# Four edits in the later stages of a six-stage transformer kernel: weight splits released earlier, a block FFN with one bank per output tile, a turned bias share, and a cross attention projected one tile later

## The reference, cut to what matters

```python
x = x + L0_xattn(layernorm(x), ctx, ctx)     # 16 heads over 1601 keys
x = x + L0_attn(layernorm(x))                # Mamba-2 like state space, 16 heads
x = x + L0_ffn(layernorm(x))                 # block-sparse FFN: below
x = x + L1_xattn(layernorm(x), ctx, ctx)     # one head: below
x = x + L1_attn(layernorm(x))                # causal self attention
x = x + L1_ffn(layernorm(x))                 # quantized FFN: below

# L0_ffn: 16 blocks of 128 hidden units, the 4 most probable of each row are kept
mask = one_hot(top_k(softmax(xf @ router_w.T + router_b), 4))
h = relu(where(mask[:, :, None], einsum('nd,ibd->nib', xf, w1b) + b1b, 0))
y = einsum('nib,dib->nd', where(mask[:, :, None], h, 0), w2b) + b2

# L1_xattn
q, k, v = query @ Wq + bq, key @ Wk + bk, value @ Wv + bv      # key = value = ctx
out = softmax(q @ k.T) @ v

# L1_ffn's weights, per block of 32 of their columns
s = max(max(abs(wb)) / 7, 1e-12);  w = clip(round(wb / s), -8, 7) * s
```

## Time and profile before

| | |
|---|---|
| device time, median of 3 runs | 1714.09 us (1713.84 to 1717.74) |
| the profiled execution: its own time | 1715.84 us |
| its span | 1714.1 us |
| PE / DVE / ACT / POOL busy, share of the span | 91% / 68% / 52% / 45% |
| end of state_space, start of block_ffn | 993.86 us |
| end of the last matmul of block_ffn | 1227.53 us |
| first instruction of the next stage | 1229.36 us |
| scores of two tiles of cross1_batches, starts at 1324.68 and 1342.05 us | 17.37 us apart |
| pause of PE between state_space and block_ffn's norm | 13.93 us |

### The profile page before, as it was taken

One profiled execution on the slowest core, in us unless ns is written; L12 is line 12 of the kernel. 1 busy time (PEld: TensorE's weight loads), 2 busy tenths in 40 slices (PEclk: granted clock), 3 DMA queues, 4 the chain that ended last, 5 costly groups with the idle time before them and its releaser, 6 DMA issues. The chain is left out here.

```text
span 1714.1 us, 33945 instructions
## 1 busy us (share of the span) xinstructions
PE 1559.1 (91%) x13873; PEld 813.7 (47%) x13982; DVE 1167.6 (68%) x1951; ACT 889.2 (52%) x1190; POOL 770.2 (45%) x384
## 2 busy tenths in 40 slices
PE   6999999999999999999799979978878989899469
PEld 3445555555555555555446453333534444444224
DVE  6688888888888888886646448987522233626981
ACT  1487777777777777776373025411211222326750
POOL 1477788888878887885204816642000000000000
PEclk9999999999999999999999969989999999999779
DMA  4589999999999999999713764558679935000001
GB/s 138 131 177 192 193 190 192 190 191 191 194 194 190 199 195 195 189 182 173 166 49 123 232 261 92 140 152 202 196 305 365 396 147 221 1 1 0 1 0 49
DMA packets 556678, 282.74 MB, mean 165 GB/s; under 512 B 482912, under 2 KB 534624, under 8 KB 553456
## 3 DMA queue, kind: packets, MB, share of 16 engines
q1 hardware_dynamic: 556528, 280.63, 69.0%
HBM read 138.74 MB, written 22.54 MB: 94 GB/s over the span
## 5 line engine op out<-in xcount | busy, mean ns | idle before, releaser
L572 POOL TENSOR_TENSOR x<-x_prob,x 128x1604 bf16<-128x1604 f32 x120 | 388.0, 3233 | 142.3 <-ACT x L737 142.3
L867 DVE TENSOR_REDUCE x_negmax<-x_score 128x1 f32<-128x1604 f32 x128 | 233.6, 1825 | 17.3 <-PE x_score L613 7.0
L727 ACT ACTIVATE x_prob<-x_score,x_negmax 128x1604 f32<-128x1604 f32 x128 | 204.8, 1600 | 25.8 <-DVE x_negmax L867 21.1
L596 PE MATMUL x_ring<-x_ctx_hi,wk_split 128*128 128x400 bf16 (+1 forms) x1024 | 216.2, 333 | 0.2 <-DVE x_kT L795 0.2
L596 PE MATMUL x_ring<-wv_split,x_ctx_hi 128*128 128x512 bf16 (+1 forms) x770 | 200.4, 379 | 9.6 <-issue 7.3
L795 DVE SCALAR_TENSOR_TENSOR x_kT<-x_ring,bk,x_kT 128x400 bf16<-128x400 f32 (+1 forms) x256 | 162.2, 634 | 31.8 <-ACT x_kT L716 23.8
L737 ACT CAST x<-x_prob 128x1604 bf16<-128x1604 f32 x120 | 182.9, 1525 | 0.0
L801 DVE TENSOR_TENSOR x_v<-x_ring,x_v 128x512 bf16<-128x512 f32 (+1 forms) x208 | 143.7, 691 | 52.9 <-ACT x_v L720 50.0
L716 ACT ACTIVATE x_kT<-x_ring,bk 128x400 bf16<-128x400 f32 (+1 forms) x196 | 116.3, 594 | 91.0 <-PE x_ring L596 90.0
L720 ACT CAST x_v<-x_ring 128x512 bf16<-128x512 f32 (+1 forms) x148 | 86.5, 585 | 96.8 <-PE x_ring L596 96.8
L596 PEld LDWEIGHTS x_ring<-x_ctx_hi,wk_split 128*128 128x128 bf16 x1024 | 93.9, 97 | 86.9 <-issue 19.7
(11 more groups left out here) (346 smaller groups left out, 2435.9 us busy)
## 6 DMA issues: line engine op xcount, KB each, us to landing
y_ctx<-in_ctx SPq DMA_DIRECT2D x16, 1664.0 KB, 10.4
y_ctxT<-in_ctxT SPq DMA_DIRECT2D x16, 1601.0 KB, 14.3
x_stage<-in_ctxT SPq DMA_DIRECT2D x48, 400.0 KB, 4.4
x_q_rows<-q_rows SPq DMA_DIRECT2D x64, 128.0 KB, 3.2
m_xT<-in_L_ffn_w SPq DMA_DIRECT2D x16, 512.0 KB, 4.5
ffn_w_parts<-m_xT SPq DMA_DIRECT2D x32, 256.0 KB, 2.6
x_stage<-in_ctxT SPq DMA_DIRECT2D x16, 401.0 KB, 5.0
f_w<-ffn_w_parts SPq DMA_DIRECT2D x4, 1024.0 KB, 8.5
```

What stands on the lines that cost most here:

```text
L572: pool.tensor_tensor(ph[:, g % 2, 1, 0:NKP], prob[:, g % 2, :], ph[:, g % 2, 0, 0:NKP], ALU.subtract).then_inc(pl_done, 1)
L596: last = pe.matmul(out_, lhs, rhs, start=(i == 0), stop=(i == len(steps) - 1))
L727: nc.scalar.activation(prob[:, g % 2, :].rearrange("p (c n) -> p c n", n=QW), scores, ACT.Exp, bias=nmax[:, g % 2:g % 2 + 1], accum_out=rs ...
L867: dve.tensor_reduce(nmax[:, pair % 2:pair % 2 + 1], scores, mybir.AxisListType.XY, ALU.max, negate=True).then_inc(max_done, 1)
```

## The change

Four edits, each in one stage.

1. In state_space POOL's split waits for the turned gates (`s_gT >= 2 * KD`), for which SP's loads already wait, and no longer for the 8 bias additions.
2. In block_ffn each output tile has a bank of its own: two that were free and the six of the hidden layer, each released when its last group was read. The first four output tiles wait for the first half of the low parts only. The next stage's weight products stand ahead of the last output tile. In Dequant POOL's multiply is gone. DVE rounds with one tensor_scalar (add, min) and one scalar_tensor_tensor (subtract, times scale). `EARLY` is 20, and the high and low parts of a later piece come one slot after its front instead of two.
3. In cross1_queries the bias share is turned by 8 small transposes into a column per tile (128x8), so that cross1_batches reads it without the loads `cqs`.
4. In cross1_batches `o` of a tile is turned after the next tile's scores (into the unused columns of `pv`), and projected after the next tile's first two turns. The addition to x moves with it, and the loop has one more step at its end.

```diff
 (state_space, gpsimd)
-            pool.wait_ge(s_xo, NT)
+            pool.wait_ge(s_gT, 2 * KD)
...
 (block_ffn)
+        out_banks = banks[0:2] + [hidden_banks[n % 6] for n in range(len(groups) - 6, len(groups))]
+        next_banks = [out_banks[n] for n in range(KD)]
...
-            dq.on_sync(sp, dq.EARLY + 6, late_weights)
+            dq.on_sync(sp, dq.EARLY + 3, late_weights)
...
-                for i in dq.fronts(n):
-                    dq.multiply_on_gpsimd(pool, i)
-            for i in range(dq.EARLY, dq.count):
-                dq.multiply_on_gpsimd(pool, i)
...
-            pe.wait_ge(s_hlo, len(groups))
-            for t in range(NT):
+            def output(t):
                 if t >= 2:
-                    pe.wait_ge(s_out, t - 1)
+                    pe.wait_ge(s_masked, len(groups) - 7 + t)
+                pe.wait_ge(s_hlo, len(groups) if t >= NT // 2 else NB)
...
+            def next_weights():
+                pe.wait_ge(s_late, 48)
+                pe.wait_ge(s_out, KD)
...
+            for t in range(NT - 1):
+                output(t)
+            next_weights()
+            output(NT - 1)
...
 (class Dequant)
-    EARLY = 17
+    EARLY = 20
...
     def turn_at(self, i):
-        return self.front_at(i) + 2
+        return self.front_at(i) + (2 if i < self.EARLY else 1)
...
-        dve.tensor_scalar(w, w, ROUND, None, ALU.add).then_inc(self.s_unit, 1)
-        dve.wait_ge(self.s_unit, 6 * i + 5)
-        dve.tensor_scalar(w, w, ROUND, 7.0, ALU.subtract, ALU.min).then_inc(self.s_unit, 1)
+        dve.tensor_scalar(w, w, ROUND, ROUND + 7.0, ALU.add, ALU.min).then_inc(self.s_unit, 1)
+        dve.wait_ge(self.s_unit, 5 * i + 5)
+        dve.scalar_tensor_tensor(blocks, blocks, ROUND, s.unsqueeze(2).broadcast_to([P, 512 // QB, QB]),
+                                 ALU.subtract, ALU.mult).then_inc(self.s_back, 1)
...
 (cross1_queries, tensor)
+            pe.wait_ge(s_row, 2)
+            for t in range(NT):
+                last = pe.transpose(banks[6][:, t:t + 1], row[:, P * t:P * t + P], ident[0:1, 0:1])
+            last.then_inc(s_col, 1)
...
 (cross1_batches, sync)
-                sp.dma_start(cqs[:, par:par + 1],
-                             cq[:, P * u:P * u + P] if one else cq[:, bass.ds(P * u, P)]).then_inc(cqs_in[par], 16)
...
 (cross1_batches, tensor: tile u)
+                if finish:
+                    pe.wait_ge(s_o, u - 1)
+                    for j in range(KC):
+                        last = pe.transpose(pv[:, CD + P * j:CD + P * j + P], o[:, P * j:P * j + P], ident[:])
+                    last.then_inc(s_to, 1)
...
                     turn(0)
                     turn(1)
+                if finish:
+                    pe.wait_ge(s_w, 16)
+                    pe.wait_ge(s_of, u - 1)
+                    if not (isinstance(u, int) and u == 2):
+                        pe.wait_ge(s_x, u - 2)
+                    for j in range(KC):
+                        last = pe.matmul(wb[:], oT[:, P * j:P * j + P], wv[:, j, :], start=(j == 0), stop=(j == KC - 1))
+                    last.then_inc(s_wo, 1)
...
                     product(2)
                     product(3).then_inc(s_pv, 1)
-                    pe.wait_ge(s_o, u)
-                    pe.wait_ge(s_tf, 5 * (u - 1) + 3)
-                    for j in range(KC):
-                        last = pe.transpose(tb[other][:, P * j:P * j + P], o[:, P * j:P * j + P], ident[:])
...
```

More of the change, by code:

```diff
@@ L1440, in _ @@
                 for j in range(KD):
-                    last = pe.matmul(banks[2 + a][:, 0:CD + 1], wqT[:, j, a * P:(a + 1) * P], wkb[:, j, :],
+                    last = pe.matmul(out_banks[KD][:, KC:KC + 1], wkb[:, j, CD:CD + 1].broadcast_to([P, P]), bq[:, j:j + 1],
                                      start=(j == 0), stop=(j == KD - 1))
                 last.then_inc(s_next, 1)
[L1444 to L1451, removed]
+            pe.wait_ge(w2_in, 16)
+            for t in range(NT - 1):
+                output(t)
+            next_weights()
+            output(NT - 1)
         @block.scalar
@@ L1770, in tile, with turn, product @@
                     last.then_inc(s_s, 1)
+                def turn(j):
+                    if j >= 2 or not (isinstance(u, int) and u == 1):
+                        pe.wait_ge(s_tf, 4 * (u - 1) + j - 1)
+                    for i, (k0, kw) in enumerate(TGROUPS[j]):
+                        last = pe.transpose(tb[j % 2][0:kw, P * i:P * i + P], prob[:, other, k0:k0 + kw], ident[:])
+                    last.then_inc(s_t, 1)
+                def product(j):
+                    pe.wait_ge(s_tf, 4 * (u - 1) + j + 1)
+                    for i, (k0, kw) in enumerate(TGROUPS[j]):
+                        for s in range(2):
+                            last = pe.matmul(pv[L * s:L * s + L, 0:CD], pT[0:kw, j, P * i + L * s:P * i + L * s + L],
+                                             cn[0:kw, other, s, 4 * j + i, :],
+                                             start=(j == 0 and i == 0), stop=(j == NTG - 1))
+                    return last
+                if finish:
[3 more added lines that the diff above has]
+                    last.then_inc(s_to, 1)
                 if products:
-                    other = 1 - par
                     n_in = 32 * ((u - 1) // 2 + 1) if isinstance(u, int) else 16 * (u + (1 if par else 0))
@@ L1804, in tile @@
                     product(3).then_inc(s_pv, 1)
-                    pe.wait_ge(s_o, u)
-                    pe.wait_ge(s_tf, 5 * (u - 1) + 3)
-                    for j in range(KC):
-                        last = pe.transpose(tb[other][:, P * j:P * j + P], o[:, P * j:P * j + P], ident[:])
-                    last.then_inc(s_t, 1)
-                    pe.wait_ge(s_tf, 5 * u)
-                    if not (isinstance(u, int) and u == 1):
-                        pe.wait_ge(s_x, u - 1)
-                    for j in range(KC):
-                        last = pe.matmul(wb[:], oT[:, P * j:P * j + P], wv[:, j, :], start=(j == 0), stop=(j == KC - 1))
-                    last.then_inc(s_wo, 1)
             each_tile(pe, tile)
@@ L1846, in _, with tile @@
         def _(dve):
-            def tile(u, par, scores, products):
+            def tile(u, par, scores, products, finish):
                 if scores:
```

137 lines of the change are left out of this document (60 added, 77 removed).

## The result

The changed kernel takes 1701.26 us, median of 7 runs, against 1714.09 us before. The ratio is 0.9925 (95% interval 0.9907 to 0.9943): 12.8 us faster, where 16.5 were forecast. The profiled execution has a span of 1702.1 us against 1714.1, at a clock of 0.962 against 0.965.

A forecast was written before the change was run, and what follows sets the result against it. PE, busy 91%, was taken as the bound, so gains come only where it stands still or runs slowly. Edits 1, 2, 3 and 4: 3.9+12.9-0.3+0 = 16.5 us off 1714.09, about 1697; own range 1692 to 1702, 8 in 10 within 1685 to 1707.

The forecast's parts named there:

- Rival B: End of state_space: additions beside POOL's splits lose 7.7 us and more, taking edit 1's 3.9; 1701 us, chance 0.15 including its opposite.
- the load stall: block_ffn: DVE's DMA wait behind the late weights, 5.9 us, was expected to stay.
- POOL's interference: block_ffn, early weight pieces: POOL's slowing of DVE, some 0.8 us per piece before, was put at 0.55.
- Rival D: block_ffn: scalar_tensor_tensor beside POOL loses 0.96 us in each of 20 pieces, 19 us in all; 1716.6 us, chance 0.05.
- R: cross1_batches: time from the products' end to the context's landing, taken as 20.0 us.
- W: cross1_batches: PE's own work per tile, taken as 16.0 us.
- T: cross1_batches: mean time per tile, (20.0+16.0)/2 = 18.0 us, against 17.37 before.
- the bound of 18.8: cross1_batches: slow bound for the tile period, making edits 3 and 4 together -6 us.
- rival C: cross1_batches: waits are worse (period 18.8 us, or the clock falls in each), 6 us more; 1703 us, chance 0.10.
- Rival A: cross1_batches: context loads are no limit, 393 GB/s only mirrors PE's pace; price +13 us, so 1684 us, chance 0.15.
- Rival E: Start of block_ffn: shorter pause holds PE's clock, 20.9 us at 0.50 shrink by up to 9; 1689 us, chance 0.10.

The follow-up runs named there:

- old_schedule: Changed kernel with only the weight-piece slots as before (17 early pieces, high and low parts two slots behind the front), new operations kept: 1713.47 us, ratio 0.9988.
- old_ops: Changed kernel with only the operations as before (two scalar operations on DVE, POOL's multiply), new slots kept: 1700.4 us, ratio 0.9911.
- undo_batches: Changed kernel with cross1_batches in its order of before, the bias-share column kept: 1691.6 us, ratio 0.986.
- early_contextT: Changed kernel, but SP issues the next tile's cT before waiting for the products that free cn: 1681.03 us, ratio 0.9798.

## Why the prediction was right or wrong

**The time** of 1697 was 4 us low; 1701.26 lies inside the forecast's own range of 1692 to 1702. Behind it stand one term that was wrong and one that was right for other reasons than given.

**Edit 1** was right in mechanism and size. The additions lost 8 times 1.07 = 8.6 us, above the 7.7 worked out from the earlier trace rows, and the stage's last addition came 5.8 us later against the 5.0 taken; the gain is 3.2 instead of 3.9. The rule of the Trainium skill that was weighed there (SBUF — State Buffer, "Who interferes with whom": the one issued first holds the shared ports for its whole instruction) agrees with this trace: 1515 to 2117 ns against 684, each addition ending 0.55 us behind the split that ran when it started, and no change where the operand lies in PSUM. Rival B, on which the prediction hung that rule, would have needed all 8.9: the rule gave the loss of an addition rightly, but part of it fell into DVE's idle time.

**Edit 2** came to 14.0 against 12.9, and the end was SP's, as said. PE's side was right: no wait, its end 216.5 us after the stage's start against 215.1 worked out. The step that failed is the load stall, carried over as 5.9 us because the late weights stay behind the same piece. The runs old_schedule and old_ops show that the stall hung on the slots: all 10 us of load waits go with the new ones. By the program's order the reason is that a slot of the four is freed by a piece's low part, which now stands one slot behind its front; that is argued, not tested by itself. DVE's last low part was 4 us earlier than worked out for it (at 1198.75), and SP took most of that back: its last store landed some 9 us later, at about 1207.8, instead of 6.4, since SP's own queue of two transposes, load and store per piece (2.6, 0.6 and 0.5 us) stood without a gap. The two errors nearly cancelled, and that the end of the stage fell within 1.5 us of the forecast is luck. The 0.26 us per piece for the new operation were right (693 ns), and so was it that they don't decide; that POOL's interference shrinks to 0.55 was never tested by itself. Rival D did not happen: of the 20 operations beside the hidden layer 19 took 0.69 us and one 1.66.

**Edit 3** was right: -0.3 in cross1_queries (less than that stage's scatter), and 3.5 us in the first tile: PE's wait there for ACT fell from 7.58 us before to 4.12 in undo_batches. The other 0.5 of the 4.0 by which undo_batches is shorter is a wait for the context that the kernel before had once.

**Edit 4** is the step that went wrong in size. The mechanism was the predicted one: the loads are issued at the products' end, R (from there to the landing) was taken as 20.0 and is 20.1, and the waits come in every second tile, with 4.4 to 5.3 us instead of 2 to 4. PE's work is W = 15.3, not 16.0, which alone would give T = 17.7. What was mis-sized is the clock behind the waits: I took 2 us for the stage, and the three scores behind a wait cost 7.5. So T is 19.2 on average, over the bound of 18.8, and edits 3 and 4 together lose 5.4 us instead of 0.3: that is rival C with its price of 6, which had been given a chance of 0.10. Rival A was wrong about the changed kernel and right about the chip: the rate is no limit at 17.4 us, since the queues move 420 GB/s in early_contextT, 16.2 us for a tile. I had read the share of 0.98 at 393 GB/s as a bound, and it left 7%.

**Rival E**, the clock at the start of block_ffn, did not happen. PE's pause fell from 13.93 to 4.97 us, and the clock is 0.50 (1.2 GHz) over 991 to 1009 all the same:

```profile
991.00:1009.00 18.00, 17.21 (x83) 16.85 (x83) 8.94 (x17) 9.26 (x17) 0.00 (x0) 0.50 1.01 410
```

Against the 16.5 us forecast edit 4 is 5.1 us worse, edit 1 0.7 worse and edit 2 1.1 better, 4.7 together. The medians show 3.7; the rest is within the scatter of the untouched stages.

## What to carry to other kernels

When work is moved from behind a point at which loads are issued to before it, the loads lose exactly that much room: move their issue in the same edit, and count the time from issue to landing against the new distance, not only the bytes against the rate. Two edits can be worth nothing or less apart and much together (156.0, 146.9 and 133.5 us here), so undoing one at a time does not show what each is worth. An instruction that gets slower beside another engine costs nothing where its engine idles: move it there rather than hold the other engine back.

## What the runs showed of the hardware that was not expected

A wait of PE of 4.4 to 5.3 us was enough for the matmuls behind it to run at a granted clock of 0.65 to 0.72 over 7.8 to 8.6 us (a mean of the two levels, 1.2 and 2.4 GHz), where the same matmuls have 1.00 without a wait: with its slow matmuls each of the three waits costs 6.7 to 7.8 us. And a DMA share of 0.98 at 393 GB/s left a little room: with an earlier issue the view shows 1.01 at 420 GB/s. That PE took a tile in 15.33 us, as if 445 GB/s had passed, does not show such a rate: the loads of each tile landed about 1 us later behind their issue than those of the tile before, so a short loop can run faster than its transfers.
